# Context attention on one core: projections one part earlier, clips in pairs, normalised rows on the scalar engine

## Chip, cores and metric

One core of a Trainium2 chip. The time is device microseconds of one launch, as the median of several runs.

## The reference

Four layers, each added to x (4 batches of 512 x 256, fp32):

```
x = x + xattn0(layernorm(x), ctx)    # first layer, "latent"
x = x + ffn0(layernorm(x))           # second layer, "experts"
x = x + xattn1(layernorm(x), ctx)    # third layer, "cross"
x = x + ffn1(layernorm(x))           # fourth layer, "self"

def xattn0(latents, context):        # 16 heads of 64, 1024 keys
    lat, ctx = layer_norm(latents, g, b), layer_norm(context, g2, b2)
    q, (k, v) = lat @ Wq, split(ctx @ Wkv)
    k = apply_rope(k, cos, sin)
    attn = softmax(clip(q @ k.T / 8, -11, 11))
    return (attn @ v) @ Wo + bo
```

The first layer normalises x twice (the layer norm outside and the one inside) and the context once; the third normalises x once and takes the context as it is.

## The kernel before

Each layer has one program per engine. For the two context layers `context_plan` writes out one list of items by hand, and every engine walks through it and executes its share of each item, in that order; semaphores join the engines. A step is one pair of heads of one batch: 8 pairs by 4 batches, 32 steps. A step has four parts of two key tiles each. In a part the plan has, in order: `front` (loads), the score items `S` of two tiles, `mid`, `behind` (the value products `AV` of the two tiles before), the clips, `tail`, the additions for the softmax sums, `late`.

What a step of the first layer needs is made in the step before. Four `kv` items (TensorE, L757 to 779, products at L716) make two key tiles of keys and values each: the scalar engine copies the values (L510), the vector engine multiplies the keys by cosine and sine (L645, L648), GpSimd adds the two into KR (L425). Two `kT` items turn KR by transposes (L786, after a wait for `rotated`), the scalar engine rounds to KH (L499), the vector engine takes the low part KL (L625). `q` is one projection of the queries. These, the transposes of the inputs (`turn`, L745) and the sums share three PSUM banks in turn, so an item on TensorE also waits for the bank of the third item before it.

For a pair of tiles the scalar engine takes the exponentials (L532), the vector engine clips each tile in place (L669) and adds the tiles up (L683, the first layer only). Four probability buffers are used in turn.

Rows are normalised by the vector engine: `stat` and `aggr` (moments, L573, L580), GpSimd's reciprocal root (L392), `newton` (four small steps, L588 to 595), `rows` (subtract the mean, multiply, in place, L601). For the first batch they stand ahead of everything; for batch b they are spread over steps 1 to 5 of batch b-1 (steps 1 to 4 in the third layer). Weights arrive in two buffers by SP's loads; `wsplit` rounds them to WH on the scalar engine (L469) and takes WL on GpSimd (L399); SP's loads of the next ones wait for that.

Of the kernel before, what the change touches and what calls it, by code (L numbers as in the profile page):

```python
# [6 lines left out]
P = 128  # L7
# [73 lines left out]
def context_plan(latent, B, NP, KT):  # L81
# [10 lines left out]
    def put(where, s, d, *items):  # L92
        where[s * parts + d] += items

    def turn(b, of, ch, g=0):
        return ("turn", b, of, ch, g)

    for s in range(steps):
        b, p = divmod(s, NP)
        more = s + 1 < steps  # L100
        if latent:
            put(tail, s, 0, ("kv", s, 3))
            put(mid, s, 1, ("kT", s, 1))
        if s > 0 and latent:
            put(tail, s, 0, ("sum", s - 1))
            put(late, s, 0, ("norm", s - 1))
# [11 lines left out]
        if latent:  # L118
            if s < 3:
                for i in range(2):  # L120
                    put(front, s, 2 * i, ("wload", 2 + 2 * s + i))
                    put(late, s, 2 * i, ("wsplit", 2 + 2 * s + i))
            if entering:
                n = b + 1
                tail[s * parts] = [("kv", s, 3), turn(n, "c", 0), ("sum", s - 1), turn(n, "c", 1)]
                put(tail, s, 1, turn(n, "x", 0), ("kv", s + 1, 0), turn(n, "x", 1))
                put(tail, s, 2, turn(n, "c", 0, 1), ("kv", s + 1, 1), turn(n, "c", 1, 1), ("q", s + 1))
            elif more:
                put(tail, s, 1, ("kv", s + 1, 0))
                put(tail, s, 2, ("kv", s + 1, 1), ("q", s + 1))  # L130
            if more:
                put(mid, s, 3, ("kT", s + 1, 0))
                put(tail, s, 3, ("kv", s + 1, 2))
            continue
# [79 lines left out]
def context_layer(nc, name, latent, x_in, x_out, context, weights, B, NP, KT):  # L214
# [21 lines left out]
    norm_steps_after, n = {}, 0  # L236
    for item in plan:
        if item[0] in ("stat", "aggr", "newton", "rows"):
            rows = QT if item[2] == "x" else KT
            n += {"stat": 2, "aggr": rows, "newton": 4, "rows": 2}[item[0]]  # L240
            norm_steps_after[item] = n
    last_turn = [max(unit[i] for i in plan if i[:2] == ("turn", b)) for b in range(B)]

    ctx = ExitStack()
    with ctx:
# [13 lines left out]
        probs = [sb(f"probs{i}", [P, 2, NQ]) for i in range(PROBS)]  # L259
# [8 lines left out]
        newton = [sb(f"newton{i}", [P, KT]) for i in range(4)]  # L268
# [21 lines left out]
        norm_steps, var_ready, rsqrt_ready = sem("norm_steps"), sem("var_ready"), sem("rsqrt_ready")  # L290
        w_high, w_split = sem("w_high"), sem("w_split")
# [160 lines left out]
        def _(act):  # L452
# [4 lines left out]
            for item in plan:  # L457
# [13 lines left out]
                elif kind == "turn":  # L471
# [86 lines left out]
        def _(dve):  # L558
            for item in plan:
# [4 lines left out]
                if kind == "stat":  # L564
# [18 lines left out]
                elif kind == "newton":  # L583
                    _, b, of, k = item
                    n = QT if of == "x" else KT
                    base = norm_steps_after[item] - 4
# [10 lines left out]
                elif kind == "rows":  # L597
                    _, b, of, k, j = item
                    rows = XN if of == "x" else C
                    for i in range(2):  # L600
                        nc.vector.tensor_scalar(rows[:, j + i, :], rows[:, j + i, :], mv[:, j + i, 0:1], newton[3][:, j + i:j + i + 1],  # L601
                                                ALU.subtract, ALU.mult).then_inc(norm_steps, 1)
# [60 lines left out]
                elif kind == "clip":  # L663
# [3 lines left out]
                    tile = probs[g % PROBS]  # L667
# [42 lines left out]
        def _(pe):  # L710
# [19 lines left out]
            for item in plan:  # L730
# [1098 lines left out]
```

## Time and profile before

| | us |
|---|---|
| median of 3 runs | 2608.24 (2607.88 to 2609.44) |
| the profiled execution | 2605.82 |
| its span, first to last instruction | 2604.0 |
| TensorE busy | 2356.7 (91%) |
| vector engine busy | 1743.8 (67%) |
| scalar engine busy | 1137.0 (44%) |
| GpSimd busy | 930.6 (36%) |

The mean granted clock of TensorE over the span is 0.939. The first layer takes about 907 us of the span, the second the time to 1079, the third to about 2100. Waits are named by the instruction that waits and by the one that released it.

### The profile page before, as it was taken

How to read it: one execution, taken by the hardware profiler on the slowest of the kernel's cores; microseconds unless marked ns; L12 is line 12 of the kernel's file. 1: busy time of each engine (PE TensorE's matmuls, PEld its weight loads, DVE VectorE, ACT ScalarE, POOL GpSimd, SP SyncE). 2: the span in 40 equal slices, each digit the busy share in tenths (PEclk: the TensorE clock that was granted, in tenths of full speed). 3: DMA queues.
4: the chain of work that ended last, by engine and by line, in shares of the span. 5: the costliest groups of instructions: out<-in, count | busy, mean ns of one | idle time of the engine just before them, and what ended most of it. 6: DMA issues, size and time to landing. Idle time of an engine off the chain costs nothing. (4 is left out here: it accounts for less than half of the span.)

```text
span 2604.0 us, 35555 instructions
## 1 busy us (share of the span) xinstructions
PE 2356.7 (91%) x13184; PEld 1504.8 (58%) x13184; DVE 1743.8 (67%) x3158; ACT 1137.0 (44%) x1806; POOL 930.6 (36%) x533
## 2 busy tenths in 40 slices
PE   5999999999999869799999999999999957989897
PEld 3555655655655557565556556655665535656565
DVE  6998798799788567555554555455445328878784
ACT  3555455455455310144453455344445513544454
POOL 3422221222122100157565666566656721100010
PEclk9999999999999978899999999999999977888887
DMA  3000000100000021310000000000000010000000
GB/s 109 19 1 25 17 1 4 38 1 1 1 17 1 10 59 45 103 45 1 1 25 17 1 1 25 17 1 1 1 17 1 1 60 9 1 1 25 17 1 25
DMA packets 62630, 48.59 MB, mean 19 GB/s; under 512 B 12226, under 2 KB 61954, under 8 KB 62466
## 3 DMA queue, kind: packets, MB, share of 16 engines
q1 hardware_dynamic: 62468, 46.40, 5.8%
q8 instruction: 105, 1.72, 0.3%
q14 instruction: 57, 0.47, 0.1%
HBM read 38.01 MB, written 8.39 MB: 18 GB/s over the span
## 5 line engine op out<-in xcount | busy, mean ns | idle before, releaser
L439 POOL TENSOR_TENSOR cross_acc_pool<-cross_acc_pool,cross_probs 128x1024 f32<-128x1024 f32 x192 | 456.9, 2380 | 55.7 <-ACT cross_probs L532 35.1
L654 DVE TENSOR_REDUCE cross_part<-cross_ring 128x1 f32<-128x512 f32 x512 | 323.9, 683 | 141.0 <-PE cross_ring L793 141.0
L425 POOL TENSOR_TENSOR latent_KR<-latent_rot 128x256 f32<-128x256 f32 x128 | 175.8, 1373 | 606.7 <-DVE latent_rot L648 606.7
L532 ACT ACTIVATE cross_probs<-cross_scores 128x1024 f32<-128x1024 f32 x256 | 249.6, 1024 | 105.0 <-PE cross_scores L826 101.0
L532 ACT ACTIVATE latent_probs<-latent_scores 128x1024 f32<-128x1024 f32 x256 | 247.5, 1019 | 86.7 <-PE latent_scores L822 86.7
L683 DVE TENSOR_TENSOR latent_acc_dve<-latent_acc_dve,latent_probs 128x1024 f32<-128x1024 f32 x192 | 257.9, 1343 | 10.0
L842 PE MATMUL cross_outT<-cross_probs,cross_VN 128*64 128x512 f32 x1024 | 255.0, 620 | 0.0
L842 PE MATMUL latent_outT<-latent_probs,latent_VN 128*64 128x512 f32 x1024 | 247.9, 605 | 0.7 <-DVE latent_probs L669 0.7
L669 DVE TENSOR_SCALAR latent_probs<-latent_probs 128x1024 f32<-128x1024 f32 x256 | 167.5, 693 | 9.4 <-ACT latent_probs L532 9.3
L793 PE MATMUL cross_ring<-cross_KH,cross_QH 64*128 64x512 f32 x512 | 141.5, 476 | 31.3 <-DVE cross_part L654 21.2
L439 POOL TENSOR_TENSOR cross_acc_pool<-cross_probs 128x1024 f32<-128x1024 f32 x32 | 76.8, 2400 | 246.6 <-PE cross_ring L854 220.6
L1130 POOL TENSOR_TENSOR self_acc_pool<-self_probs 128x1024 f32<-128x1024 f32 x16 | 39.5, 2468 | 349.2 <-ACT self_probs L1192 349.2
L716 PE MATMUL latent_ring<-latent_WH,latent_CTH 128*128 128x256 f32 x512 | 157.6, 308 | 0.0
L510 ACT ACTIVATE latent_VN<-latent_ring 128x256 f32<-128x256 f32 x128 | 49.2, 384 | 248.1 <-PE latent_ring L716 248.1
L716 PEld LDWEIGHTS latent_ring<-latent_WH,latent_CTH 128*128 128x128 f32 x512 | 96.7, 189 | 96.2 <-issue 96.1
L627 DVE SCALAR_TENSOR_TENSOR cross_KL<-cross_ring,cross_bqkv,cross_KH 128x512 fp32r<-128x512 f32 x64 | 47.9, 751 | 149.9 <-ACT cross_KH L502 149.8
L716 PE MATMUL latent_ring<-latent_WL,latent_CTH 128*128 128x256 f32 x512 | 144.5, 282 | 0.0
L716 PE MATMUL latent_ring<-latent_WH,latent_CTL 128*128 128x256 f32 x512 | 144.0, 281 | 0.0
L793 PEld LDWEIGHTS cross_ring<-cross_KH,cross_QH 64*128 64x128 f32 x512 | 62.7, 186 | 134.7 <-issue 66.9
L842 PEld LDWEIGHTS cross_outT<-cross_probs,cross_VN 128*64 128x64 f32 x1024 | 63.5, 139 | 107.1 <-issue 87.3
L842 PEld LDWEIGHTS latent_outT<-latent_probs,latent_VN 128*64 128x64 f32 x1024 | 62.1, 136 | 108.2 <-issue 105.8
L822 PE MATMUL latent_scores<-latent_QH,latent_KH 64*128 64x512 f32 x512 | 114.6, 443 | 1.8 <-issue 1.6
(294 smaller groups left out, 5532.6 us busy)
## 6 DMA issues: line engine op xcount, KB each, us to landing
latent_C<-in_ctx_dram SPq DMA_DIRECT2D x4, 1024.0 KB, 6.5
cross_C<-in_ctx_dram SPq DMA_DIRECT2D x4, 1024.0 KB, 6.9
latent_XN<-in_x_dram SPq DMA_DIRECT2D x4, 512.0 KB, 3.9
latent_WRAW<-in_L_xattn_Wkv_dram SPq DMA_DIRECT2D x16, 128.0 KB, 2.5
latent_X<-in_x_dram SPq DMA_DIRECT2D x4, 512.0 KB, 3.8
x_after<-latent_X SPq DMA_DIRECT2D x4, 512.0 KB, 2.9
experts_raw<-in_L_ffn_expert_w_dram SPq DMA_DIRECT2D x1, 2048.0 KB
experts_XN<-x_after SPq DMA_DIRECT2D x4, 512.0 KB, 3.9
```

The source lines that it names most:

```text
L425: nc.gpsimd.tensor_tensor(KR[:, 2 * t:2 * t + 2, :], rot1s[n % 2][:, :, :], rot2s[n % 2][:, :, :], ALU.add)\
L439: nc.gpsimd.tensor_tensor(acc_pool[:, :, :], first[:, :, :], probs[g % PROBS][:, :, :], ALU.add)\
L510: nc.scalar.activation(VN[s % 2][:, 2 * t:2 * t + 2, :], src[:, :, 128:256], ACT.Copy).then_inc(v_copied, 1)
L532: nc.scalar.activation(probs[g % PROBS][:, :, :], scores[g % 2][:, :, :], ACT.Exp, scale=SCALE)\
L627: nc.vector.scalar_tensor_tensor(out=L[:, cols], in0=bank[:, :], scalar=bqkv[:, bias, p:p + 1], in1=H[:, cols].bitcast(fp32), op0=ALU.add, ...
L654: nc.vector.reduce_max(part[:, qt, h, i:i + 1], bank[:, :], AX.X).then_inc(taken, 1)
L669: nc.vector.tensor_scalar(tile[:, :, :], tile[:, :, :], exp(CLIP), exp(-CLIP), ALU.min, ALU.max)\
L683: nc.vector.tensor_tensor(acc_dve[:, :, :], first[:, :, :], probs[g % PROBS][:, :, :], ALU.add)\
L716: last = nc.tensor.matmul(out, still, moving, start=i == 0, stop=i == len(passes) - 1)
L793: nc.tensor.matmul(bank[:, :], QH[s % QBUF][HEAD[h], qt * P:(qt + 1) * P], KH[s % 2][HEAD[h], i * 512:(i + 1) * 512], start=True, stop=Tru ...
L822: last = nc.tensor.matmul(scores[g % 2][:, h, :], k[s % 2][HEAD[h], ks], q[s % QBUF][HEAD[h], :], start=i == 0, stop=latent and i == 2)
L842: last = nc.tensor.matmul(outT[HEAD[h], :], V[:, t, at + h * DH:at + (h + 1) * DH], probs[g % PROBS][:, h, :], start=t == 0, stop=t == KT - 1)
```

## The change

Four edits. The first three concern the first layer, the fourth both context layers.

1. Each `kv` item goes one part earlier: items 0 to 3 of step s+1 stand in parts 0 to 3 of step s (before: in parts 1 to 3 of step s and part 0 of step s+1). Item 3 of step 0 goes ahead of the first step. In the last step of a batch, whose successor has new inputs, item 0 stays in part 1, item 1 in part 2, items 2 and 3 stand in part 3.
2. `kT` items go from `mid` to `tail`, behind the value products: item 1 from part 1 to part 0, item 0 of the next step from part 3 to part 2 (part 3 in the last step of a batch). `q` goes from part 2 to part 1, except there. A `kv` item now waits on TensorE for the split of its weights.
3. Two probability tiles are clipped by one instruction of 2048 columns, which waits for the second exponential. The four buffers become one tensor.
4. `rows` go to the scalar engine, in place, as scale times row plus shift. A fifth small step of `newton` makes the shift, -mean x scale. TensorE's transposes and the next round's statistics wait for a new semaphore, `rows_ready`.

```diff
-            put(tail, s, 0, ("kv", s, 3))
-            put(mid, s, 1, ("kT", s, 1))
...
             if entering:
                 n = b + 1
-                tail[s * parts] = [("kv", s, 3), turn(n, "c", 0), ("sum", s - 1), turn(n, "c", 1)]
+                before_sum, behind_sum = [turn(n, "c", 0)], [turn(n, "c", 1)]
                 put(tail, s, 1, turn(n, "x", 0), ("kv", s + 1, 0), turn(n, "x", 1))
                 put(tail, s, 2, turn(n, "c", 0, 1), ("kv", s + 1, 1), turn(n, "c", 1, 1), ("q", s + 1))
+                put(tail, s, 3, ("kT", s + 1, 0), ("kv", s + 1, 2), ("kv", s + 1, 3))
             elif more:
-                put(tail, s, 1, ("kv", s + 1, 0))
-                put(tail, s, 2, ("kv", s + 1, 1), ("q", s + 1))
-            if more:
-                put(mid, s, 3, ("kT", s + 1, 0))
-                put(tail, s, 3, ("kv", s + 1, 2))
+                before_sum = [("kv", s + 1, 0)]
+                put(tail, s, 1, ("kv", s + 1, 1), ("q", s + 1))
+                put(tail, s, 2, ("kT", s + 1, 0), ("kv", s + 1, 2))
+                put(tail, s, 3, ("kv", s + 1, 3))
+            put(tail, s, 0, ("kT", s, 1), *before_sum, *[("sum", s - 1)] * (s > 0), *behind_sum)
...
-        plan += [("q", 0)] + [("kv", 0, t) for t in range(2)] + [("kT", 0, 0), ("kv", 0, 2)]
+        plan += [("q", 0)] + [("kv", 0, t) for t in range(2)] + [("kT", 0, 0), ("kv", 0, 2), ("kv", 0, 3)]
...
+                elif kind == "rows":
+                    _, b, of, k, j = item
+                    rows = XN if of == "x" else C
+                    act.wait_ge(norm_steps, norm_steps_after["newton", b, of, k])
+                    for i in range(j, j + 2):
+                        last = nc.scalar.activation(rows[:, i, :], rows[:, i, :], ACT.Identity, scale=newton[3][:, i:i + 1],
+                                                    bias=shifts[:, i:i + 1])
+                    last.then_inc(rows_ready, 1)
...
                     if base and j == 0:
                         dve.wait_ge(norm_steps, base)
+                        dve.wait_ge(rows_ready, rows_before[item])
...
                     dve.wait_ge(norm_steps, base + 4)
-                elif kind == "rows":
...
-                        nc.vector.tensor_scalar(rows[:, j + i, :], rows[:, j + i, :], mv[:, j + i, 0:1], newton[3][:, j + i:j + i + 1],
-                                                ALU.subtract, ALU.mult).then_inc(norm_steps, 1)
+                    nc.vector.scalar_tensor_tensor(out=shifts[:, 0:n], in0=mv[:, 0:n, 0], scalar=-1.0, in1=newton[3][:, 0:n],
+                                                   op0=ALU.mult, op1=ALU.mult).then_inc(norm_steps, 1)
...
-                elif kind == "clip":
+                elif kind == "clip" and item[2] % 2 == 1:
...
+                    both = all_probs[:, (g - 1) % PROBS:g % PROBS + 1, :, :].rearrange("p t h n -> p (t h n)")
                     dve.wait_ge(exp_done, g + 1)
-                    nc.vector.tensor_scalar(tile[:, :, :], tile[:, :, :], exp(CLIP), exp(-CLIP), ALU.min, ALU.max)\
-                      .then_inc(clipped, 1)
+                    nc.vector.tensor_scalar(both, both, exp(CLIP), exp(-CLIP), ALU.min, ALU.max).then_inc(clipped, 2)
...
-                        pe.wait_ge(norm_steps, norm_steps_after["rows", b, of, int(latent and of == "x"), n - 2])
+                        pe.wait_ge(rows_ready, rows_before["rows", b, of, int(latent and of == "x"), n - 2] + 1)
...
                         what, cols = slice(1, 3), slice(p * P, (p + 1) * P)
+                        pe.wait_ge(w_split, p + 1)
```

## Rows read from the trace of the kernel before

**Rows 1.** Busy us by stretch: length, PE, PEld, DVE, ACT, POOL; granted clock, DMA share, GB/s.

```profile
63.00:880.00 817.00, 786.85 (x4756) 477.17 (x4756) 710.14 (x1245) 417.43 (x598) 202.70 (x143) 1.00 0.03 10
65.00:170.00 105.00, 99.14 (x604) 58.34 (x602) 100.52 (x193) 55.86 (x83) 40.18 (x28) 1.00 0.04 12
695.00:880.00 185.00, 180.36 (x1084) 108.08 (x1082) 151.54 (x235) 90.44 (x128) 40.22 (x28) 1.00 0.02 7
```

**Rows 2.** Waits of TensorE, 60 to 905 us: total, times, longest.

```profile
PE latent_ring L786 <- POOL latent_KR L425: 27.1, 32, 1.3
```

**Rows 3.** The same waits, 65 to 170 us, then 695 to 880 us.

```profile
PE latent_ring L786 <- POOL latent_KR L425: 4.5, 4, 1.3
...
PE latent_ring L786 <- POOL latent_KR L425: 4.6, 7, 1.0
```

**Rows 4.** Timeline of TensorE, one step: start, busy time, instruction.

```profile
166.55 0.50 PE L822 MATMUL latent_scores<-latent_QH,latent_KH 64*128 64x512 f32 x2
...
168.14 1.94 PE L842 MATMUL latent_outT<-latent_probs,latent_VN 128*64 128x512 f32 x8
...
170.00 0.39 PE L716 MATMUL latent_ring<-latent_WH,latent_CTH 128*128 128x256 f32 x1
...
171.42 0.28 PE L716 MATMUL latent_ring<-latent_WH,latent_CTL 128*128 128x256 f32 x1
...
171.63 1.08 PE L854 MATMUL latent_ring<-latent_acc_dve,latent_ones 128*64 128x512 f32 x4
...
172.64 0.50 PE L822 MATMUL latent_scores<-latent_QH,latent_KH 64*128 64x512 f32 x2
...
175.49 0.63 PE L786 MATMUL latent_ring<-latent_ident,latent_KR 128*128 128x128 f32 x4 [1.19 <-POOL latent_KR L425]
```

**Rows 5.** Timeline of the vector engine, the same step.

```profile
166.06 1.29 DVE L669 TENSOR_SCALAR latent_probs<-latent_probs 128x1024 f32<-128x1024 f32 x2
...
171.60 1.29 DVE L669 TENSOR_SCALAR latent_probs<-latent_probs 128x1024 f32<-128x1024 f32 x2
...
172.81 0.42 DVE L645 TENSOR_TENSOR latent_rot<-latent_ring,latent_cos 128x256 f32<-128x256 f32 x1
```

**Rows 6.** Timeline of GpSimd, the same step.

```profile
161.31 0.73 POOL L425 TENSOR_TENSOR latent_KR<-latent_rot 128x256 f32<-128x256 f32 x1 [3.75 <-DVE latent_rot L648]
...
173.71 1.64 POOL L425 TENSOR_TENSOR latent_KR<-latent_rot 128x256 f32<-128x256 f32 x1 [3.91 <-DVE latent_rot L648]
```

**Rows 7.** Groups by line, scalar engine, first layer: count, busy us, mean ns.

```profile
L510 ACT ACTIVATE latent_VN<-latent_ring 128x256 f32<-128x256 f32 x128 | 49.2, 384 | 248.1 <-PE latent_ring L716 248.1
...
L499 ACT ACTIVATE latent_KH<-latent_ring 128x512 fp32r<-128x512 f32 x64 | 38.6, 603 | 6.5 <-PE latent_ring L786 6.2
...
L481 ACT ACTIVATE latent_staging<-latent_ring,latent_gbc 128x512 f32<-128x512 f32 x16 | 12.4, 778 | 12.0 <-DVE latent_XTL L609 9.3 <-PE latent_ring L745 2.3
```

**Rows 8.** Timeline of all engines, start of the first layer.

```profile
8.07 0.16 DVE L588 TENSOR_TENSOR latent_newton<-latent_rstd 128x4 f32<-128x4 f32 x1 [1.21 <-POOL latent_rstd L392]
...
8.87 1.38 DVE L601 TENSOR_SCALAR latent_XN<-latent_XN,latent_mv,latent_newton 128x256 f32<-128x256 f32 x4
...
21.19 3.84 POOL L399 TENSOR_TENSOR latent_WL<-latent_WRAW,latent_WH 128x384 fp32r<-128x384 f32 x4
...
21.26 0.94 DVE L588 TENSOR_TENSOR latent_newton<-latent_rstd 128x8 f32<-128x8 f32 x1 [1.81 <-POOL latent_rstd L392]
...
25.09 2.84 DVE L601 TENSOR_SCALAR latent_C<-latent_C,latent_mv,latent_newton 128x256 f32<-128x256 f32 x8
...
29.14 0.78 ACT L481 ACTIVATE latent_staging<-latent_ring,latent_gbc 128x512 f32<-128x512 f32 x1 [9.34 <-DVE latent_XTL L609]
```

**Rows 9.** Timeline of all engines, start of the third layer.

```profile
1090.10 1.38 DVE L601 TENSOR_SCALAR cross_XN<-cross_XN,cross_mv,cross_newton 128x256 f32<-128x256 f32 x4
...
1090.46 0.94 ACT L469 ACTIVATE cross_WH<-cross_WRAW 128x384 fp32r<-128x384 f32 x2 [6.60 <-DMA cross_WRAW<-in_L_xattn_Wv_dram]
...
1092.97 1.23 ACT L486 ACTIVATE cross_XTH<-cross_ring 128x512 fp32r<-128x512 f32 x2
```

More of the change, by code:

```diff
@@ L100, in context_plan @@
         more = s + 1 < steps
-        if latent:
-            put(tail, s, 0, ("kv", s, 3))
-            put(mid, s, 1, ("kT", s, 1))
-        if s > 0 and latent:
-            put(tail, s, 0, ("sum", s - 1))
+        if latent and s > 0:
             put(late, s, 0, ("norm", s - 1))
@@ L122, in context_plan @@
                     put(late, s, 2 * i, ("wsplit", 2 + 2 * s + i))
+            before_sum, behind_sum = [], []
             if entering:
                 n = b + 1
-                tail[s * parts] = [("kv", s, 3), turn(n, "c", 0), ("sum", s - 1), turn(n, "c", 1)]
+                before_sum, behind_sum = [turn(n, "c", 0)], [turn(n, "c", 1)]
                 put(tail, s, 1, turn(n, "x", 0), ("kv", s + 1, 0), turn(n, "x", 1))
                 put(tail, s, 2, turn(n, "c", 0, 1), ("kv", s + 1, 1), turn(n, "c", 1, 1), ("q", s + 1))
+                put(tail, s, 3, ("kT", s + 1, 0), ("kv", s + 1, 2), ("kv", s + 1, 3))
             elif more:
-                put(tail, s, 1, ("kv", s + 1, 0))
-                put(tail, s, 2, ("kv", s + 1, 1), ("q", s + 1))
-            if more:
-                put(mid, s, 3, ("kT", s + 1, 0))
-                put(tail, s, 3, ("kv", s + 1, 2))
+                before_sum = [("kv", s + 1, 0)]
[3 more added lines that the diff above has]
+            put(tail, s, 0, ("kT", s, 1), *before_sum, *[("sum", s - 1)] * (s > 0), *behind_sum)
             continue
@@ L235, in context_layer @@
     rounds = {item: n + 1 for n, item in enumerate(i for i in plan if i[0] == "aggr")}
-    norm_steps_after, n = {}, 0
+    norm_steps_after, rows_before, n, done = {}, {}, 0, 0
     for item in plan:
-        if item[0] in ("stat", "aggr", "newton", "rows"):
+        if item[0] in ("stat", "aggr", "newton"):
             rows = QT if item[2] == "x" else KT
-            n += {"stat": 2, "aggr": rows, "newton": 4, "rows": 2}[item[0]]
+            n += {"stat": 2, "aggr": rows, "newton": 5}[item[0]]
             norm_steps_after[item] = n
+        rows_before[item] = done
+        done += item[0] == "rows"
     last_turn = [max(unit[i] for i in plan if i[:2] == ("turn", b)) for b in range(B)]
@@ L258, in context_layer @@
         QH, QL = ([sb(f"Q{part}{i}", [P, NQ], f32r) for i in range(QBUF)] for part in "HL")
-        probs = [sb(f"probs{i}", [P, 2, NQ]) for i in range(PROBS)]
+        all_probs = sb("probs", [P, PROBS, 2, NQ])
+        probs = [all_probs[:, i, :, :] for i in range(PROBS)]
         acc_dve = sb("acc_dve", [P, 2, NQ]) if BY_DVE else None
@@ L267, in context_layer @@
         varr, rstd, carrier = sb("varr", [P, KT]), sb("rstd", [P, KT]), sb("carrier", [P, 1])
-        newton = [sb(f"newton{i}", [P, KT]) for i in range(4)]
+        newton, shifts = [sb(f"newton{i}", [P, KT]) for i in range(4)], sb("shifts", [P, KT])
         if latent:
@@ L290, in context_layer @@
         norm_steps, var_ready, rsqrt_ready = sem("norm_steps"), sem("var_ready"), sem("rsqrt_ready")
+        rows_ready = sem("rows_ready")
         w_high, w_split = sem("w_high"), sem("w_split")
@@ L585, in _ @@
                     n = QT if of == "x" else KT
-                    base = norm_steps_after[item] - 4
+                    base = norm_steps_after[item] - 5
                     dve.wait_ge(rsqrt_ready, rounds["aggr", b, of, k])
@@ L596, in _ @@
                     dve.wait_ge(norm_steps, base + 4)
-                elif kind == "rows":
-                    _, b, of, k, j = item
-                    rows = XN if of == "x" else C
-                    for i in range(2):
-                        nc.vector.tensor_scalar(rows[:, j + i, :], rows[:, j + i, :], mv[:, j + i, 0:1], newton[3][:, j + i:j + i + 1],
-                                                ALU.subtract, ALU.mult).then_inc(norm_steps, 1)
+                    nc.vector.scalar_tensor_tensor(out=shifts[:, 0:n], in0=mv[:, 0:n, 0], scalar=-1.0, in1=newton[3][:, 0:n],
+                                                   op0=ALU.mult, op1=ALU.mult).then_inc(norm_steps, 1)
                 elif kind == "turn":
@@ L662, in _ @@
                                                 -1.0 / DH, None, ALU.mult).then_inc(max_steps, 1)
-                elif kind == "clip":
+                elif kind == "clip" and item[2] % 2 == 1:
                     _, s, t = item
                     g = tile_no(s, t)
-                    tile = probs[g % PROBS]
+                    both = all_probs[:, (g - 1) % PROBS:g % PROBS + 1, :, :].rearrange("p t h n -> p (t h n)")
                     dve.wait_ge(exp_done, g + 1)
-                    nc.vector.tensor_scalar(tile[:, :, :], tile[:, :, :], exp(CLIP), exp(-CLIP), ALU.min, ALU.max)\
-                      .then_inc(clipped, 1)
+                    nc.vector.tensor_scalar(both, both, exp(CLIP), exp(-CLIP), ALU.min, ALU.max).then_inc(clipped, 2)
                 elif kind == "add" and item[2] in BY_DVE[1:]:
```

## Prediction

> **What bounds the kernel now.** I read the busy time by stretch first. In the first attention layer (63 to 880 us) TensorE is busy 786.9 of 817 us at a granted clock of 1.00, its 2.4 GHz level [rows 1]; so this stage ends when TensorE is through, and all that can be won there is the 30 us in which it stands still. Then the waits of TensorE: between 60 and 905 us it waits 32 times, once a step, 27.1 us in all, for GpSimd's KR, the rotated keys, before it turns them (L786) [rows 2]. Nothing else comes near. Third, the same wait by stretch: 4.5 us in 4 waits between 65 and 170 us, where the vector engine also normalises the next batch, and 4.6 us in 7 waits in the last batch, where it doesn't [rows 3]. That is 1.1 to 1.3 us a step against 0.66. The vector engine is busy 100.5 of 105 us in the first of these stretches and 151.5 of 185 us in the second [rows 1]: nearly a second bound in the one, with room in the other.
>
> The timeline of one step shows where the wait comes from [rows 4, 5, 6]. The last product of the fourth kv block starts at 171.42 and ends at 171.70; the copy of the values takes 0.38 [rows 7], so the rotation could start at about 172.1, but the vector engine is still clipping and starts it at 172.81, 0.7 late. It takes 0.8; GpSimd's addition starts at 173.71 and takes 1.64 beside the additions of the vector engine (0.73 where that waits, at 161.31) [rows 6]. Meanwhile TensorE has the sum (1.01) and two score tiles (1.59); it is through at 174.30 and waits 1.19 until 175.49 [rows 4]. The chain is 0.6 longer than its cover even when the vector engine is on time.
>
> **Steady part, order.** Each kv block moves one part (a quarter step) forward, and the keys are turned behind the value products. Work is moved, none is added. Before the second turn of a step TensorE will have two score tiles and two value tiles: the sum (1.01) leaves the cover and the value products (168.14 to 170.00, 1.86) enter it, 0.85 us more [rows 4]. In steps without normalisation the wait of 0.66 then goes entirely, with 0.2 to spare. For the first turn of a step the cover grows as well (a query block and the same four tiles); today it doesn't wait. What is late next is the second turn again, in the steps where the vector engine is late.
>
> **Steady part, load of the vector engine.** The normalised rows leave it: 2.84 us for eight, 0.35 each [rows 8]. Clipping two tiles at once saves the start of one instruction: today a pair takes 1.21 from its first start to the next instruction (171.60 to 172.81) [rows 5]. No row shows a 2048-element clip; between no saving and 0.2 a pair I take 0.07, because 0.60 a tile is mostly stream: 9 us in all over 128 pairs, none of it on the path by itself. In the stretch 65 to 170 the eight latent rows (2.8 to 3.7 us) and about 16 pairs (1.1) leave 96 us of work, while the stretch shrinks by at most its 4.5 us of waits to 100.5: the vector engine stays at 95%. So there the lateness remains, and grows as TensorE catches up with it. In these steps (the second to fifth of the first three batches, 12 in all) today's 1.2 less 0.85 gives 0.35 as the lower end, 1.2 (nothing won) is the upper; I take 0.8, since the engine's share of the step doesn't fall. That leaves 12 x 0.8 = 9.6 us. Won: 27.1 - 9.6 = **17.5 us**.
>
> **Pairs.** A pair waits for its second exponential. Today a pair is clipped by 167.35 and TensorE asks for it at 168.14 [rows 4, 5]: 0.79 to spare. The pair's end hardly moves, only its first tile is ready 0.6 later, when nobody asks yet. Cost 0 while that slack holds; bound 0.6 a part if it is gone (below).
>
> **Scalar engine in the steady part.** A copy of 256 columns takes 0.38 there, and scale and bias given as columns add 0.778 - 0.603 = 0.18 (both groups have 512 columns) [rows 7]. So I price a row at 0.56, or 0.46 from start to start, as neighbours overlap by about 0.1. 48 rows of the later batches make 22 us on an engine busy 417 of 817 us [rows 1]; they come in pairs behind the copy of the values, so at most about 1 us ahead of an exponential that has 2 us before its clip matters. Cost 0. The new wait of statistics for rows_ready, in front of the whole vector queue, is met a part earlier; the wait of the kv blocks for w_split is met a step earlier, though all of TensorE stands behind it.
>
> **Start of the layer.** Here nothing covers. Two rounds of x: four rows by the vector engine take 1.38 [rows 8]; by the scalar engine 3 x 0.46 + 0.56 = 1.94, plus the new shifts instruction (0.2) and the hand-over (0.1): +0.8 each, +1.6. The context round: its four Newton steps take 21.26 to 25.09, 3.83, because GpSimd splits weights beside them from 21.19; the x round's take 0.8 [rows 8]. The split now comes later, as the scalar engine rounds the weights after its rows; five steps take 1.0: -2.8. Eight rows: 7 x 0.46 + 0.56 = 3.8 against 2.84: +1.0. Rows are done 0.2 early, near 27.7. But then the scalar engine has both weight roundings (2 x 0.94, the same shape in the later layer [rows 9]) and the x transposes (four at 0.78 less the overlap of 0.1), which today lie ahead of 29.14 [rows 8]; the context staging starts near 32.2, **+3.0**. Bounds +1 and +5: the split may collide with the low parts. SP's next weight loads wait for the split, which ends near 32.4 instead of 25.0; their use is a step away. One kv block (170.00 to 171.63, 1.63 [rows 4]) also moves from the last step ahead of the first: 0, bounds -1.6 and +1.6.
>
> The page "ScalarE: Activation LUTs" of the Trainium skill (section "Rules for kernel authors") says to give multiplications and additions to the vector engine, which speaks against this edit; its section "What ACT_TABLE_LOAD costs" gives, as an estimate, 585 ns for such a row and 492 from start to start; by it the start would cost 0.4 us more. No row before shows this instruction.
>
> **Third layer.** Its one x round costs +0.8: rows that start at 1090.10 today, and take 1.38, end near 1092.3. The rounding of the transposed x, at 1092.97 now, then comes behind both weight roundings, 0.94 each, which run beside the rows today, from 1090.46 [rows 9]. They end near 1094.2: **+1.3**, bounds 0 and +3. Later batches: 0, the rows are needed many parts later.
>
> **Sum.** -17.5 + 3.0 + 1.3 = -13.2. The profiled execution took 2605.82 us (span 2604.0), so 2592.6; the median of the runs is 2608.24, 2.4 above it, so **2595.0**.
>
> **The rivals.**
> - The wait goes altogether (0.16): the vector engine's relief is enough in all steps. For it: 0.85 of cover and lighter work together exceed 1.2. Against: 95% busy. -27.1 + 4.3 = -22.8: 2585.4.
> - The vector engine sets the time in the 12 steps (0.17): they keep 1.2 each, 14.4 us, only the other 12.7 go: -12.7 + 4.3 = -8.4: 2599.8. For it: its share [rows 1].
> - The change does not do what it says (0.10): the wait moves along with the rotation, because its chain lengthens by what the cover gains, and only start costs remain: 2612.5, no change. For it: GpSimd's 0.73 to 1.64 [rows 6].
> - Slower (0.07): value products wait for pairs. It decides when a pair ends over 0.79 later, relative to TensorE, than today. Then the first tile, ready 0.6 sooner today, is missed in each part; in the 4 parts of the 12 full steps 48 x 0.6 = 28.8: 2623.8. Against it: the slack, and that rows leave the queue ahead of the clips.
>
> **How the numbers follow.** The forecast has 0.50. The range runs from the first rival with a start of +1 (2583) to the second with the dear ends of both starts (2605); outside lie the third and fourth rival and 0.03 of tails. Of about 0.2% (5.2 us), which is what a measurement here can tell from no change, faster means below 2603.0: 0.50 + 0.16 + 0.15 = 0.81; the same 0.12; slower 0.07.
>
> **What would show it.** Right: TensorE's wait at the turning of keys falls from 27.1 to about 10 us and is left in the normalising steps; the 63 to 880 stretch shortens by about 17; the context staging starts near 32; the rows take 0.56 on the scalar engine; clips take about 1.2 for 2048 elements. Wrong: value products that wait for clips; a wait for KR in the last batch; a start over 5 us later; a lower granted clock in the first layer.

## The result, and the profile after

The changed kernel takes 2544.89 us (median of 3 runs, 2544.38 to 2545.72) against 2608.24: a ratio of 0.9756, 95% interval 0.9734 to 0.9779. The forecast was 2595.0 with a range of 2583 to 2605. The direction was right, the size was not: 63 us were won where 13 were forecast. The profiled execution has a span of 2542.9 us (2604.0 before).

Where they went, by the queue's store and load issues (a layer from its start to the issue of its last store):

| stretch | before | after | difference | forecast |
|---|---|---|---|---|
| first layer | 906.5 | 876.5 | -30.1 | -14.5 |
| second layer | 172.4 | 170.2 | -2.2 | 0 |
| third layer | 1033.8 | 1004.7 | **-29.1** | +1.3 |
| fourth layer | 488.0 | 488.3 | +0.3 | 0 |

(The third layer starts at its load of x, the second and fourth where the one before ended.) The second layer's code is the same; it took 169.8 to 172.9 us over all kernels below, so its 2.2 belong to no cause. Half of the gain lies in the third layer, where nothing was forecast.

**First layer.** Of the changed kernel, first the waits of TensorE from 60 to 905 us (total, times, longest), then from 65 to 170 us; these answer to [rows 2] and [rows 3].

```profile
PE latent_outT L849 <- DVE latent_probs L676: 3.9, 3, 1.8
PE latent_ring L793 <- POOL latent_KR L427: 3.7, 8, 0.7
...
PE latent_ring L793 <- POOL latent_KR L427: 1.8, 3, 0.7
```

The wait for the rotated keys falls from 27.1 to 3.7, not to about 10; value products wait for clips three times, 3.9 in all (0.7 before), which the forecast had named as a sign against itself. The busy times by stretch, columns as in [rows 1]:

```profile
65.00:170.00 105.00, 101.13 (x632) 60.33 (x630) 100.76 (x176) 62.34 (x96) 44.67 (x30) 1.00 0.04 12
695.00:850.00 155.00, 154.64 (x954) 90.16 (x952) 137.43 (x186) 86.33 (x120) 35.48 (x25) 1.00 0.02 8
```

In the last batch TensorE is now busy 154.6 of 155 us. In the normalising stretch of the first batch the vector engine is as busy as before, 100.8 of 105 us against 100.5. The wait for the keys falls there from 4.5 to 1.8, but 2.1 of the waits for clips are new, so TensorE stands still for 3.9 us of it (5.9 before). In the second and in the third batch 0.8 of the wait is left each. Next the groups of the rows on the scalar engine and of the clips (count, busy, mean ns):

```profile
L494 ACT ACTIVATE latent_XN<-latent_XN,latent_shifts,latent_newton 128x256 f32<-128x256 f32 x24 | 13.0, 591 | 1.4 <-DVE latent_shifts L608 1.4
...
L676 DVE TENSOR_SCALAR latent_probs<-latent_probs 128x2048 f32<-128x2048 f32 x126 | 154.7, 1228 | 22.9 <-ACT latent_probs L542 22.9
```

A row takes 0.59 (0.56 was assumed), a pair of clips 1.23 as one instruction (before, two took 1.29 together [rows 5]). The start of the layer on the scalar engine:

```profile
23.96 4.04 ACT L494 ACTIVATE latent_C<-latent_C,latent_shifts,latent_newton 128x256 f32<-128x256 f32 x8 [6.55 <-DVE latent_shifts L608]
27.90 1.75 ACT L471 ACTIVATE latent_WH<-latent_WRAW 128x384 fp32r<-128x384 f32 x4
...
32.48 0.78 ACT L483 ACTIVATE latent_staging<-latent_ring,latent_gbc 128x512 f32<-128x512 f32 x1 [0.16 <-DVE latent_XTL L616]
```

The context staging starts at 32.48, 3.3 after the 29.14 of [rows 8]; 3.0 was forecast.

**Third layer.** Waits of TensorE over the layer, first of the kernel before (1082 to 2116 us), then of the changed one (1049 to 2054 us):

```profile
PE cross_ring L793 <- DVE cross_part L654: 21.2, 13, 3.3
PE cross_ring L745 <- DVE cross_XN L601: 13.9, 1, 13.9
```

```profile
PE cross_ring L751 <- ACT cross_XN L494: 14.9, 1, 14.9
...
PE cross_ring L800 <- DVE cross_part L661: 3.4, 7, 0.8
```

TensorE waited 21.2 us for maxima of the vector engine, and waits 3.4 now; the wait for the first rows grew by 1.0. From output copy to output copy, six of the layer's 32 steps were long before: 33.75, 32.66, 32.75, 28.96, 33.88 and 32.74 us. After, all six take 27.40 to 27.45: 30.2 us less. TensorE has the same 164 products in each; in the six together it stood still for 18.8 us before and 0.7 after, and was busy 175.9 us before and 163.9 after. So 18.1 of the 30.2 are waits, and 12.1 are products that took longer, at a granted clock of 0.90 to 0.95 in five of the six steps, 1.00 after. They are two steps in each of the three batches that normalise the next one's rows, those with the `rows` items.

### The profile page after: what moved, and what is told of

Read it like the earlier page. It is cut to its first block and busy times, and to the rows that moved or that the text cites. A ratio compares the mean times of both kernels' runs of the same rounds, so it can differ in the third digit from the quotient of the medians.

```text
span 2542.9 us, 35559 instructions
## 1 busy us (share of the span) xinstructions
PE 2332.5 (92%) x13184; PEld 1499.3 (59%) x13184; DVE 1694.5 (67%) x2966; ACT 1180.1 (46%) x1886; POOL 934.1 (37%) x533
## 5 line engine op out<-in xcount | busy, mean ns | idle before, releaser
L849 PE MATMUL cross_outT<-cross_probs,cross_VN 128*64 128x512 f32 x1024 | 247.8, 605 | 0.0
L676 DVE TENSOR_SCALAR latent_probs<-latent_probs 128x2048 f32<-128x2048 f32 x128 | 157.8, 1233 | 25.3 <-ACT latent_probs L542 25.3
```

What stands on the lines that cost most here:

```text
L676: nc.vector.tensor_scalar(both, both, exp(CLIP), exp(-CLIP), ALU.min, ALU.max).then_inc(clipped, 2)
L849: last = nc.tensor.matmul(outT[HEAD[h], :], V[:, t, at + h * DH:at + (h + 1) * DH], probs[g % PROBS][:, h, :], start=t == 0, stop=t == KT - 1)
```

## Experiments: one part at a time

The change has three parts for the first layer (order, rows, clips), and the rows are also the third layer's. Three kernels put one each into the kernel before (all three also have the changed kernel's wait for `w_split`, and the fifth Newton step and `rows_ready` even where the rows stay with the vector engine); a fourth takes the third layer's rows out of the changed kernel.

**Order alone** (`e1_order`): the plan's part of the diff and the wait for `w_split`, in short

```diff
-            put(mid, s, 1, ("kT", s, 1))
...
-                put(mid, s, 3, ("kT", s + 1, 0))
...
+                put(tail, s, 2, ("kT", s + 1, 0), ("kv", s + 1, 2))
...
+            put(tail, s, 0, ("kT", s, 1), *before_sum, *[("sum", s - 1)] * (s > 0), *behind_sum)
...
+                        pe.wait_ge(w_split, p + 1)
```

> The kernel before with the new order of the first layer alone (each kv block and the keys' second turn a part earlier or behind the value products, one kv block moved ahead of the first step); rows and single clips stay with the vector engine. The first layer, from the start to the issue of its last store, took 906.5 us before and 876.5 after; the third, from its load of x to its last store, 1033.8 and 1004.7. Theory (the order alone wins the first layer): its steps without normalisation fall from 24.52 to about 23.5 us, those with it from 25.1-25.5 to at most 24.3; the first layer lands at 874 to 880 (the start costs only the moved block of 1.63), the third stays at 1033 to 1035, the whole run at 2574 to 2582. Rival (the relief of the vector engine by rows and clips is what took the wait away in the normalising steps): these 12 steps stay near 25 us, the first layer lands at 887 to 893, the whole at 2588 to 2595.

Measured: 2582.49 us; first layer 882.0, third 1033.6. Plain steps 23.49. The normalising steps came out between the two theories, 23.5 to 25.5 and one of 26.0, and so did the first layer. TensorE's waits, 60 to 905 us:

```profile
PE latent_ring L802 <- POOL latent_KR L427: 13.4, 16, 1.5
```

The order wins 24.5 us, and leaves 13.4 of wait in 16 places where the vector engine is late. That is near the 9.6 that the forecast left there; so what took the rest away in the changed kernel must be another part.

**Rows alone** (`e2_rows`): the scalar engine's branch, the shifts and `rows_ready`, with the old order and single clips.

```diff
+                elif kind == "rows":
...
+                        last = nc.scalar.activation(rows[:, i, :], rows[:, i, :], ACT.Identity, scale=newton[3][:, i:i + 1],
+                                                    bias=shifts[:, i:i + 1])
+                    last.then_inc(rows_ready, 1)
```

> The kernel before with the normalised rows on the scalar engine in the first and third layer, and nothing else. Theory (the third layer's gain of 29.1 us comes from the rows leaving the vector engine, where two rows took up to 5 us beside GpSimd's additions): the third layer falls from 1033.8 to 1004 to 1006 and its six long steps (33.75, 32.66, 32.75, 28.96, 33.88, 32.74) return to 27.4; the first layer, whose order is the old one, changes by -4 to +3; the whole lands at 2573 to 2583. Rival one (the third layer gained from something else, such as its later start or the order): it stays near 1033 and the whole near 2605. Rival two (the first layer's normalising steps suffered from the rows as well): the first layer falls by over 8 and the whole below 2570.

Measured: 2578.86 us; third layer 1005.2, all six long steps at 27.4; first layer 907.6. The third layer's gain belongs to the rows alone. In the first layer they win nothing with the old order: the wait falls only to 23.7, the first step ends 4.9 later, and the steps behind it win 3.9 of that back.

**Clips alone** (`e3_clips`): the one instruction over two tiles.

```diff
+                elif kind == "clip" and item[2] % 2 == 1:
...
+                    nc.vector.tensor_scalar(both, both, exp(CLIP), exp(-CLIP), ALU.min, ALU.max).then_inc(clipped, 2)
```

> The kernel before with clips by pairs of tiles alone. A pair of clips took 1.21 us and takes 1.23 as one instruction. Theory: the clip saves nothing on the vector engine, the first layer stays within 3 us of 906.5 and the whole within 4 us of 2608. Rival one (one instruction less per part is what relieved the vector engine): normalising steps fall by about 0.7 us each and the first layer by 8 or more, the whole to 2600 or less. Rival two (the first tile of each pair is now late for its value product): each step with a late vector engine grows by about 0.6 a part, 28 us in all, the whole near 2636.

Measured: 2607.83 us, ratio 0.9996 (0.9984 to 1.0007); first layer 907.8, third 1034.5. Alone they are worth nothing that can be measured.

**Third layer's rows back** (`e4_rows3_back`):

```diff
-                elif kind == "rows":
+                elif kind == "rows" and latent:
```

in the scalar engine's branch; the vector engine has its old instruction for the rest, counted by `rows_ready`.

> The changed kernel with the normalised rows of the third layer back on the vector engine, the first layer as changed. Theory (rows beside GpSimd's additions): the third layer returns from 1004.7 to 1032 to 1035, with six steps of 29 to 34 us in place of 27.4; the first stays at 876.5; the whole lands at 2571 to 2576 (2544.9 and 29, less about 1 at the layer's start). Rival (its gain came from elsewhere): the whole stays at 2544 to 2547.

Measured: 2577.05 us (2573.69 to 2580.41); third layer 1035.7, the six steps at 34.2, 32.8, 32.8, 29.0, 34.0 and 32.8; first layer 875.2. About a microsecond above the numbers given, and the rival is out.

## Experiments: why the third layer's rows were dear

The later batches' rows wait for nothing, and nobody waits for them. Two kernels keep the rows on the scalar engine and put two idle instructions at the same places in the vector engine's queue, the third layer's later batches only. They add work that the reference has not; its result is read by nobody.

```diff
+                elif kind == "rows" and not latent and item[1]:
...
+                    for i in range(2):
+                        nc.vector.bn_stats(spare_stats[:, i, :], bo[:, :])
```

```diff
+                        nc.vector.tensor_scalar(spare[:, i, :], bo[:, :], mv[:, i, 0:1], newton[3][:, i:i + 1], ALU.subtract, ALU.mult)
```

The first is `e7_idle_stats`, the second, in the same loop, `e8_idle_scale`.

> The changed kernel (rows on the scalar engine), and in the third layer, at each place where the later batches' rows stand in the vector engine's queue, two statistics instructions over a constant row of 256, whose result nobody reads: the same engine, place, count and columns as the two rows before, but a form that took 0.41 us beside GpSimd's additions in the kernel before. Theory (the rows waited for GpSimd's additions, and only therefore the maxima were late): 0.8 us a place is covered, the third layer stays within 3 us of 1004.7, the whole at 2543 to 2548. Rival (any work of the vector engine at that place makes the maxima late): 10 to 30 us come back, the whole lands at 2555 to 2575.

> As the run with idle statistics, but with the very form of the rows (subtract and multiply by two columns, 256 elements from memory to memory) over the same constant row into a spare tile. Theory (this form waits for GpSimd's additions): each of the 12 takes up to 2.6 us in place of 0.35, the six steps of 29 to 34 us are back, the third layer lands at 1030 to 1036, the whole at 2570 to 2577. Rival (the loss came from who waits for the rows, not from the instruction): the third layer stays near 1005, the whole near 2545.

Measured: with statistics 2546.89 us and a third layer of 1006.3; with scalings 2578.58 us, 1.6 above the range given, and 1035.7. The tile's own view (minimum, median and maximum of the 12, in ns), with statistics and then with scalings:

```profile
L614 DVE BATCH_NORM_STATS2 cross_spare_stats<-cross_bo x12: 407/412/420, 1200.1 to 1703.4; 128x6 f32<-128x256 f32 x12
```

```profile
L614 DVE TENSOR_SCALAR cross_spare<-cross_bo,cross_mv,cross_newton x12: 401/1359/2561, 1200.6 to 1726.2; 128x256 f32<-128x256 f32 x12
```

The same engine, place, count and columns: one form always takes 0.41, the other up to 2.56. The kernel before shows the same spread on the rows themselves, and it stood there to be read (the mean of these twelve is 1.74):

```profile
L601 DVE TENSOR_SCALAR cross_XN<-cross_XN,cross_mv,cross_newton x12: 400/1298/2560, 1232.7 to 1758.3; 128x256 f32<-128x256 f32 x12
```

The trace shows what the long ones wait for. Eleven of the twelve, in both of these runs, end 0.15 or 0.16 us after an addition of GpSimd ends, and GpSimd's next addition starts only as the scaling ends. The twelfth falls between two additions and takes 0.40, and the four rows of the first batch, with no addition beside them, take 0.41 each. All twelve pieces of statistics lie inside an addition and take 0.41 to 0.42. So the long time of a scaling is mostly a wait, which the profile counts as busy time. Two rows of one place together took up to 3.9 us, not the 5 of the expectation above.

What happens behind them shows in the timelines of the run with scalings, of the vector engine, GpSimd and TensorE:

```profile
1200.57 3.84 DVE L614 TENSOR_SCALAR cross_spare<-cross_bo,cross_mv,cross_newton 128x256 f32<-128x256 f32 x2
1204.33 2.47 DVE L666 TENSOR_REDUCE cross_part<-cross_ring 128x1 f32<-128x512 f32 x4
...
1191.77 14.97 POOL L442 TENSOR_TENSOR cross_acc_pool<-cross_acc_pool,cross_probs 128x1024 f32<-128x1024 f32 x6
...
1205.06 0.79 PE L805 MATMUL cross_ring<-cross_KH,cross_QH 64*128 64x512 f32 x1 [3.41 <-DVE cross_part L666]
1205.78 3.68 PE L854 MATMUL cross_outT<-cross_probs,cross_VN 128*64 128x512 f32 x8
...
1211.90 1.94 PE L854 MATMUL cross_outT<-cross_probs,cross_VN 128*64 128x512 f32 x8
```

GpSimd adds with hardly a pause, one addition every 2.5 us, from 1191.8 to 1206.7. Two scalings among them take 3.84 in place of 0.7; the four maxima behind them start that much later, TensorE waits 3.41 for a bank, and its next eight value products take 3.68 where they take 1.94 six microseconds later. By stretch, with the granted clock behind the five busy times:

```profile
1205.00:1210.50 5.50, 5.44 (x12) 1.97 (x13) 2.39 (x6) 0.00 (x0) 1.74 (x1) 0.50 0.00 0
```

After the stall the granted clock stands at 0.50, the 1.2 GHz level. So a step loses twice: the wait, and a stretch at the lower level behind it. This step took 33.76 us where the changed kernel takes 27.40. The rule of the Trainium skill that bears on it is that of the page "SBUF — State Buffer", section "SBUF: two separate sides": vector engine and GpSimd share a pair of ports as an exclusive lock, and whichever starts first keeps it for its whole instruction. This trace agrees: the longest scaling, 2.56, is as long as an addition (2.38 in the mean) and a little. That page reckons instructions with two operands in memory among those that wait, too; the start of the first layer agrees, with a Newton step of 0.91 in place of 0.17 (below).

The statistics were not free either: the six steps take 28.1 (0.7 more, 4.0 in all; the layer shows only 1.6 of it, because its last step came out 1.5 shorter), and TensorE's wait for maxima is 5.1 instead of 3.4. Some 13% of the loss of 30.2 comes from any work at that place, the rest from the form, which has to wait for additions.

## Experiments: the first layer's parts together

**Single clips again** (`e6_clips_back`) and **the first layer's rows on the vector engine again** (`e5_rows1_back`), each in the changed kernel:

```diff
-                elif kind == "clip" and item[2] % 2 == 1:
+                elif kind == "clip":
...
-                elif kind == "rows":
+                elif kind == "rows" and not latent:
```

> The changed kernel with single clips in place of pairs. Pairs alone, put into the kernel before, left the first layer at 907.8 us (906.5), 2.2 of it lost in the first step and 0.7 in the last. Theory (pairs are worth nothing once the rows are gone): the first layer lands at 873 to 878, the whole at 2541 to 2547, with the first step about 2 us shorter. Rival (the relief in the normalising steps, from 24.7 and 25.0 with the new order alone to 23.5 and 24.0, needs rows and clips together): the normalising steps grow by 0.3 or more each and the first layer lands at 880 to 883, the whole near 2550.

> The changed kernel with all normalised rows of the first layer back on the vector engine (order and pairs of clips stay). The order alone took the first layer to 882.0 us, with the rows on the scalar engine 879.1, with rows and pairs 876.5. Theory (pairs relieve the vector engine only a little; the rows' 2.84 us per eight are what the normalising steps need, and the scalar engine gives 3.75 of it back at the start): first layer 878.5 to 881, its first step ends near 70.2, its normalising steps keep 24.3 to 25.0; the whole at 2546 to 2551. Rival (with pairs the rows no longer matter): normalising steps of 23.5 to 24.1, first layer near 872.5, the whole near 2541.

Measured: 2547.73 and 2548.44 us. All kernels together, profiled execution. The wait is TensorE's for the rotated keys, 60 to 905 us; the first step ends where its output copy starts; the steady part goes from the end of that copy to the end of the last step's.

| kernel | wait, times | first step ends | steady part | first layer | third layer |
|---|---|---|---|---|---|
| before | 27.1, 32 | 68.4 | 815.1 | 906.5 | 1033.8 |
| clips | 25.4, 32 | 70.6 | 814.5 | 907.8 | 1034.5 |
| rows | 23.7, 32 | 73.3 | 811.2 | 907.6 | 1005.2 |
| order | 13.4, 16 | 70.3 | 789.6 | 882.0 | 1033.6 |
| order, rows | 7.3, 10 | 73.7 | 782.6 | 879.1 | 1004.0 |
| order, clips | 7.2, 16 | 68.5 | 785.8 | 876.7 | 1004.9 |
| all three | 3.7, 8 | 74.0 | 780.2 | 876.5 | 1004.7 |

The steady part repeats well: the five kernels here whose first layer is the changed kernel's have 779.9 to 780.3. With the old order the clips take 1.7 off the wait and the rows 3.4, with the new order 6 each: there the chain is covered unless the vector engine is late, so that relief turns into time. In the steady part the clips win 0.6 with the old order, 3.8 behind the new one, and 2.4 behind order and rows. They save busy time of the vector engine: in the run with single clips, of the changed kernel's order, their group reads

```profile
L676 DVE TENSOR_SCALAR latent_probs<-latent_probs 128x1024 f32<-128x1024 f32 x252 | 166.6, 698 | 13.6 <-ACT latent_probs L542 13.6
```

against 154.7 for the pairs above, 12 us less for the vector engine. The first layer of `e6` fell between its theory and its rival, that of `e5` 1.8 under its theory and 4.2 above its rival. In `e5` the first step ended at 68.5 us, not 70.2, at a granted clock of 1.00 between 40 and 45 us; `e9` below has the same start, a clock of 0.69 there, and a first step of 70.1. So such a dip costs about 1.6 us there. The changed kernel has one too (0.67 between 45 and 50 us); run again, without the dip, its first step ends at 73.1 in place of 74.0 and its first layer takes 875.0 in place of 876.5.

So in the first layer the scalar engine's rows are worth little: 876.7 us without them, 875.0 with them, both without a dip. They win 5.6 in the steady part and give 4.6 back at the start, where nothing covers them. The medians differ by more, 2548.44 against 2544.91 for the changed kernel on the same chip, but over half of the difference of the two profiled executions lies in the second and the fourth layer, whose code is the same in both.

**The place of the turns** (`e11_turns_mid`). A plain step is 1.03 shorter than before, and only 0.66 of it was a wait.

```diff
-                put(tail, s, 2, ("kT", s + 1, 0), ("kv", s + 1, 2))
+                put(tail, s, 2, ("kv", s + 1, 2))
...
-            put(tail, s, 0, ("kT", s, 1), *before_sum, *[("sum", s - 1)] * (s > 0), *behind_sum)
+            if more:
+                put(mid, s, 3, ("kT", s + 1, 0))
+            put(mid, s, 1, ("kT", s, 1))
+            put(tail, s, 0, *before_sum, *[("sum", s - 1)] * (s > 0), *behind_sum)
```

> The changed kernel with both turns of the keys put back between the score and the value products, where the kernel before had them, while the kv blocks stay a part earlier, so that no turn waits for the rotated keys. The plain steps took 24.52 us before, 23.49 now, where a wait of 0.61 to 0.66 a step went. Theory (the place of a turn has a price: four transposes took 0.55 to 0.59 us between scores and value products and 0.41 between value products and a kv block): plain steps near 23.85, the first layer longer by 10 to 13 us (886 to 890), the whole at 2555 to 2559. Rival (the missing 0.4 a step is the wait itself, dearer than recorded): plain steps stay at 23.49, the whole at 2544 to 2546.

Measured: 2554.72 us. Plain steps 23.89, all of them; first layer 884.1, under what was given because its first step ended 2.3 sooner. From the end of the first step to that of the 31st it takes 773.9 us, the changed kernel 764.0, the kernel before 798.2. So of the 34.2 us that this stretch lost, 9.9 are the place of the turns. They are busy time: TensorE is busy 767.0 us in this stretch here, 756.7 in the changed kernel and 768.6 in the kernel before. The timeline of TensorE, in this run and then in the changed kernel:

```profile
754.20 0.66 PE L796 MATMUL latent_ring<-latent_ident,latent_KR 128*128 128x128 f32 x4
754.79 0.65 PE L852 MATMUL latent_outT<-latent_probs,latent_VN 128*64 128x512 f32 x2
```

```profile
780.38 0.66 PE L793 MATMUL latent_ring<-latent_ident,latent_KR 128*128 128x128 f32 x4
780.79 0.36 PE L722 MATMUL latent_ring<-latent_WH,latent_CTH 128*128 128x256 f32 x1
```

Four transposes hold the queue 0.59 us between scores and value products, and 0.41 between value products and a kv block (these are also the medians over all turns of the two runs; 0.56 in the kernel before). Twice a step that is 0.36 of the 0.40. Why the neighbour matters was not tried.

## Experiments: a faster start

**First batch's rows on the vector engine** (`e9_first_rows`):

```diff
-                elif kind == "rows":
+                elif kind == "rows" and item[1] > 0:
```

with the vector engine's old instruction for batch 0.

> The changed kernel with the first batch's rows, in both layers, back on the vector engine, where nothing covers them; the later batches' rows stay on the scalar engine. In the first layer the first step ended at 74.0 us in the changed kernel, at 70.3 with the new order and the vector engine's rows. Theory (the scalar engine's rows are what made the starts longer): the first step ends near 70.3 to 72.6, the third layer starts 1 us sooner, and the whole lands at 2539 to 2543. Rival (the pairs of clips in the first step cost it): the first step stays at 73 or later and the whole at 2544 or more.

Measured: 2541.84 us; first step at 70.1, first layer 873.8, third 1003.6. At its start, the fourth Newton step of the context round and GpSimd's weight splits:

```profile
24.42 0.91 DVE L606 TENSOR_TENSOR latent_newton<-latent_newton,latent_rstd 128x8 f32<-128x8 f32 x1
...
21.47 3.84 POOL L401 TENSOR_TENSOR latent_WL<-latent_WRAW,latent_WH 128x384 fp32r<-128x384 f32 x4
```

**The start reordered** (`e10_start`), on top of it; and the changed kernel again beside it (`e12_changed_again`):

```diff
+    turn_x = [turn(0, "x", ch) for ch in range(2)]
+    if latent:
+        behind_x, behind_aggr = plan.index(("stat", 0, "c", 0, 0)), plan.index(("newton", 0, "c", 0))
+        plan = plan[:behind_x] + plan[-2:] + plan[behind_x:behind_aggr] + turn_x + plan[behind_aggr:-2]
...
-        plan += [("q", 0)] + [("kv", 0, t) for t in range(2)] + [("kT", 0, 0), ("kv", 0, 2), ("kv", 0, 3)]
+        plan += [("q", 0)] + [("kv", 0, t) for t in range(3)] + [("kT", 0, 0), ("kv", 0, 3)]
...
+                    if latent and p == 0:
+                        pool.wait_ge(rows_ready, rows_before[item])
```

The last two lines hold GpSimd's weight splits until the rows of x are done; `nsin` is held until those of the context are.

> A version meant to be faster than both: the first batch's rows of both layers on the vector engine (2541.8 so, 2544.9 with the scalar engine), and the start of the first layer reordered: GpSimd's two weight splits, which blocked the context round's Newton steps (0.92 us each where they take 0.2), run beside the statistics of the context rows; the low parts of x come ahead of those Newton steps; a third kv block comes ahead of the first turn of the keys, which waited 2.3 us. Theory: rounding of the turned context starts near 26.4 us (29.7 in the run with the first rows back), the first step ends near 65 to 66.5 (70.1), the whole lands at 2536 to 2539. Rival (the splits only move the collision, to the statistics or to the low parts): the first step ends at 69 or later, the whole at 2541 or more.

> The changed kernel itself once more, beside the version with the reordered start on the same chip: 2543 to 2547.

Measured: 2538.03 us (2535.71 to 2539.31), the changed kernel beside it 2544.91 (2542.89 to 2548.17). Against the kernel before the ratios are 0.9726 (0.9713 to 0.9739) and 0.9760 (0.9747 to 0.9773). The first step ends at 64.4, the first layer takes 867.4.

```profile
16.12 3.87 POOL L408 TENSOR_TENSOR latent_WL<-latent_WRAW,latent_WH 128x384 fp32r<-128x384 f32 x4 [2.56 <-DVE latent_XN L623]
...
22.75 0.17 DVE L614 TENSOR_TENSOR latent_newton<-latent_newton,latent_rstd 128x8 f32<-128x8 f32 x1
...
27.04 0.78 ACT L491 ACTIVATE latent_staging<-latent_ring,latent_gbc 128x512 f32<-128x512 f32 x1 [7.00 <-PE latent_ring L767]
```

Beside the statistics of the context rows the splits take 3.87 and hold up little (the instruction behind the statistics takes 0.49 in place of 0.17); a Newton step takes 0.17 in place of 0.91. The staging starts at 27.04, 0.6 later than expected and 2.7 sooner than in `e9`. Of the 5.7 us by which the first step ends sooner than there, some 1.6 are the dip of the clock that `e9` had and this run has not. This version is faster than the changed kernel beside it. Against `e9`, two runs on another chip, it is 3.8 us ahead, which these runs alone do not show to be more than scatter.

## Why the prediction was wrong

- **Third layer, "Later batches: 0, the rows are needed many parts later"**: the step that failed, 30.2 us. It asked who waits for the rows, not what stands behind them on the vector engine and how long they take there. The rows cost up to 2.56 each beside GpSimd's additions and delayed the maxima behind them, and TensorE paid 18.1 us in waits and 12.1 in slower products. That GpSimd could hold up the vector engine stood in the forecast itself, for the first layer's Newton steps (3.83 instead of 0.8).
- **"All that can be won there is the 30 us in which it stands still"; order, what a plain step wins**: 0.66 a step was about right for the wait (0.61 in a plain step), and 1.03 was measured. The other 0.4 is the place of the turns, 9.9 us in all, a term that the sum did not have. "Work is moved, none is added" took a moved instruction to cost the same everywhere. From the end of the first step to that of the 31st TensorE's idle time fell by 22.3 us and its busy time by 11.9.
- **Steady part, load of the vector engine, 12 x 0.8 = 9.6 left**: 3.7 was left in 8 waits, and the waits of value products for clips grew by 3.2. With the order alone 13.4 is left, so the residue was rightly seen; that the relief could not help "since the engine's share of the step doesn't fall" was wrong. The share indeed stayed (96% before and after in the stretch from 65 to 170 us, 94% in the second batch's normalising steps), and most of the lateness went: an engine that is nearly always busy can still be on time where it is asked for. The normalisation is spread over five steps of each of the three batches, so 15 steps, not 12.
- **Pairs, 0.07 saved**: 12 us of the vector engine over 126 pairs, 0.09 each; about right. That none of it is on the path held with the old order only.
- **Rows on the scalar engine, 0.56 and 0.46 from start to start**: 0.59, and (4.04 - 0.59) / 7 = 0.49. The estimate from the page of the Trainium skill that the forecast named beside it ("ScalarE: Activation LUTs", section "What ACT_TABLE_LOAD costs") was nearer with 585 and 492 ns. By that estimate the start comes out 0.5 us dearer, not the 0.4 that the forecast gave.
- **Start of the first layer, +3.0**: +3.3 to the staging, right, and by the path that was given: the five Newton steps took 1.0, the rows ended at 28.0 (27.7 was forecast), the roundings and the x transposes followed. The split did collide with the low parts, as the bounds allowed: two of them took 2.75 in place of 1.28. The first step ended 5.7 later. The 3.3 and the 1.63 of the kv block moved ahead make 4.9; the repeat without a dip of the clock has 4.7, and the dip costs the other 1.0. The last step, which lost that block, is only 0.7 shorter. The stretch behind it, whose code is unchanged, varies from 21.0 to 22.5 us over all runs.
- **Third layer's start, +1.3**: the rounding of the transposed x stands 11.88 after the layer's load, 10.71 before: +1.2, right.
- The rival that the wait goes altogether was nearest in the first layer. None had the third layer, nor the place of the turns.

## What to carry to other kernels

Moving work off an engine is to be priced by what stands behind it in that engine's queue, in every layer that shares the code: compare the shortest and the longest of a group, for a mean four times the shortest (here 1.74 against 0.40) can be a wait that no view of waits lists. Where GpSimd adds at length, keep scalings from memory to memory off the vector engine, or put them where GpSimd rests. Parts of a change whose chains meet are tested together as well as alone: here rows and clips left the first layer no shorter by themselves, and took 5.5 us off it behind the new order.

## What the runs showed of the hardware

- Beside GpSimd's additions of 2.38 us a scaling of 256 elements took 0.40 to 2.56 us and ended, 11 times of 12, 0.15 or 0.16 after an addition; the statistics of the same 256 elements took 0.41 to 0.42. The wait stands in the profile as busy time.
- Behind a stall of 3.41 us the granted clock of TensorE was 0.50 in the next 5.5 us, and eight value products took 3.68 in place of 1.94.
- Four transposes held TensorE's queue for 0.59 us between score and value products and for 0.41 between value products and a kv block.
